# Two places for the query tiles, another order of score tiles, and new step times in an attention layer's hand-written order

## The chip, the cores and the metric

One NeuronCore of a Trainium2 chip runs the whole program. Its engines are TensorE (PE, with its weight loads as PEld), VectorE (DVE), ScalarE (ACT), GpSimd (POOL) and SyncE (SP), whose queue issues every DMA here. The metric is the device time of one execution in microseconds (us).

## The reference

A transformer layer on x of 2 x 1024 x 512: latent attention with 32 heads, then a gated feed-forward, each between layer norms and added to x. All in float32.

```
q = rms_norm(x @ wq_a.T, q_norm_w) @ wq_b.T            # 32 heads of 128 + 64
q_pe = rope(q[..., 128:]);  kv = x @ wkv_a.T
k_pe = rope(kv[..., 64:]);  k_nope, v = rms_norm(kv[..., :64]) @ wkv_b.T
scores = (q_nope . k_nope + q_pe . k_pe) * scale, causal
out = softmax(scores) @ v @ wo.T
x = x + layernorm(attn(layernorm(x)))
x = x + layernorm((silu(h @ w_gate.T) * (h @ w_up.T)) @ w_down.T)   # h = layernorm(x)
```

## The kernel before

Every float32 product is made of three on rounded halves (high x high, high x low, low x high; `three`). The attention works in the latent space: keys are 128 rows (64 latent, 64 rotary) shared by all heads, so each head needs its queries (two halves c of 512 tokens), its scores, its probabilities times the latents, and, per pair of heads, a transpose of the results that are then multiplied by a folded matrix of values and output weights.

A **job** is one tile of 128 queries of one head; there are 64 heads (2 batches x 32) of 8 jobs, in the order `TILES`. Tile j sees (j+1) x 128 keys. For a job PE makes the scores in one of four places of PSUM (`s_ps`: 1, 2, 2 and 1 banks, job i in place i % 4), DVE takes the `minimum` (L1371), ACT the `exponential` (L1168) and `split_high` (L1176, into pk), DVE `split_low` (L1384), after which the place is free for job i + 4. Two neighbouring jobs have 9 blocks of 128 x 128 together, a **pair** u; SP sends the pair through a transposing DMA from pk (NPK = 3 places) to pt (NPT = 4 places) (`turn_probs`, L772), PE multiplies it with the latents (`values`, L987, 18 matmuls of 130 columns into o_ps), DVE inverts the sums (`invert_sums`), ACT scales (`outputs_norm`, L1185), POOL adds two halves into o_pair (`outputs_add`, L1578), PE transposes them (`outputs_turn`, L996), and ACT and DVE split them into ot_high (L1194) and ot_low (L1391).

The queries of head n are made while head n - 1 runs. For each half PE makes a product (L116, x_ps<-qa...,weff_in), ACT copies it to q_raw (`queries_raw`, L1158), two DMAs of SP swap its rotary rows into qs (`queries_swap`, L782), and POOL turns and splits it in five steps (`queries_turn`): qf = raw x cos (L1548), qs = qs x sin (L1551), qf + qs (L1554), q_high (L1559), q_low (L1561). q_raw, qf and qs have one place each, so the second half waits for the first: ACT for the first half's cos and swap, SP for its L1554.

The products with the folded matrix (`output`, L116, x_ps<-m_in,ot...) come once for four heads (a group), eight of them, spread over the next group; their sums are taken by DVE (L1407) or ACT (L1213). In the second batch m_in is loaded again from memory, 1 MB for a group (`output_load`, L791); in the first it is made beside the heads (`fold_values`, L1004) and stored.

All products but scores and values go through one bank, x_ps, which each of them takes only when its predecessor was read (`take_bank`). Every engine executes its part of one list in order. The list is sorted by **steps**, one step a job: scores of job i stand at step i, everything else at a step plus a delay from the tables at the file's head. A line such as

```
for u in range(NJ // 2):
    at(2 * u + 1 + TURN_PROBS, "turn_probs", u)
    step = 2 * u + 1 + VALUES
```

puts the transpose of pair u behind its second job. A step says nothing of time: it only says what stands ahead of what in each engine's row. At the end the first token work of the feed-forward is mixed in between the last output products (EARLY_START, EARLY_EVERY).

Of the kernel before, what the change touches and what calls it, by code (L numbers as in the profile page):

```python
# [35 lines left out]
NX, NA, NPK, NPT, NON = 4, 3, 3, 4, 8  # L36
# [14 lines left out]
O_STEPS = (4.97, 7.03)
AFTER_OUTPUT = dict(output_add=0.36, output_store=1.5)
FOLD_STEP = 1.07
AFTER_FOLD = dict(fold_high=0.02, fold_low=1.08, fold_store=1.5)
END_STEP, END_EVERY = 9.71, 1.38
# [10 lines left out]
EARLY_START, EARLY_EVERY = 6.94, 0.84  # L66

PACES = (7, 3, 4)
# [12 lines left out]
TILES = (1, 6, 4, 3, 0, 7, 5, 2)  # L81
# [50 lines left out]
class Signals:  # L132


    def __init__(self, new):
# [23 lines left out]
        self.q_mm, self.q_raw, self.q_swap, self.q_cos, self.q_sin = (  # L159
            new(n) for n in ("q_mm", "q_raw", "q_swapped", "q_cos", "q_sin"))  # L160
# [268 lines left out]
def attention_order(end):  # L429
# [858 lines left out]
def vector_program(e, M, S):  # L1288
    w = Waits(e)
    def latents_begin():  # L1290
        e.memset(M.eps1[:, 0:1], LN_EPS)
# [218 lines left out]
def gpsimd_program(e, M, S):  # L1510
# [189 lines left out]
```

## Time and profile before

| | us |
|---|---|
| median of three executions | 1716.17 |
| lowest, highest | 1712.88, 1717.09 |
| the profiled execution, time | 1718.1 |
| its span | 1716.3 |
| PE busy | 1572.2 (92%) |
| DVE, ACT, POOL busy | 1147.7, 1069.0, 952.9 |

The span runs from the first instruction to the last; the time is 1.8 us longer. A share of busy time is a mean over stages: about 96 us that make the latents, then the attention, a change-over, and the feed-forward. Matmul records overlap their neighbours, so a PE that is called busy can still start its matmuls late.

### The profile page before, as it was taken

The numbers are of one execution on the slowest core, as the hardware profiler recorded it, in microseconds if no ns is written. First come the engines' busy times: TensorE is split into PE (matmuls) and PEld (weight loads), VectorE is DVE, ScalarE is ACT, GpSimd is POOL, SyncE is SP. The second block draws the span as 40 slices with busy tenths as digits, with TensorE's granted clock in tenths as the row PEclk, the third lists the DMA queues.
The fourth block names the chain that finished last, engine by engine and source line by source line (L and its number), as shares of the span: only waits on it lengthen the run. The fifth ranks groups of instructions, "written<-read, shape, count | busy, mean of one in ns | idle before, by whom it ended". The sixth has DMA issues, their size and how long they took to land.

```text
span 1716.3 us, 30452 instructions
## 1 busy us (share of the span) xinstructions
PE 1572.2 (92%) x10720; PEld 1275.9 (74%) x10720; DVE 1147.7 (67%) x2548; ACT 1069.0 (62%) x2159; POOL 952.9 (56%) x911
## 2 busy tenths in 40 slices
PE   5878999999998999998999999999978899999997
PEld 5856777778777777777877777777766677888775
DVE  6866677777777777776777777777766542323356
ACT  5677777777777777777877777777754433212122
POOL 2556677677676677676767677677622321111132
PEclk9899999999999999999999999999998999999998
DMA  8669999998999989899889898988996300201022
GB/s 280 227 140 206 164 200 181 189 200 174 203 175 190 180 190 201 184 187 188 171 172 190 164 179 169 183 171 165 184 186 239 121 25 1 74 1 39 1 92 80
DMA packets 661095, 268.84 MB, mean 157 GB/s; under 512 B 608432, under 2 KB 619184, under 8 KB 658768
## 3 DMA queue, kind: packets, MB, share of 16 engines
q1 hardware_dynamic: 660944, 266.90, 72.0%
q8 instruction: 86, 1.41, 0.3%
q14 instruction: 65, 0.53, 0.1%
HBM read 69.70 MB, written 29.36 MB: 58 GB/s over the span
## 4 chain that ended last, share of the span: by engine, by line
PE 56%; DMA 14%; DVE 11%; ACT 6%; POOL 6%; issue 4%; SPq 2%; POOLq 0%; ACTq 0%; DVEq 0%
PE f_ps L116 14%; PE s_ps L973 12%; PE x_ps L116 11%; DMA pt<-pk 10%; PE o_ps L987 9%; PE fd_ps L116 6%; DMA qs<-q_raw 3%; DVE pk L1384 3%; PE x_ps L996 2%; DVE s_ps L1371 1%; POOL q_low L1561 1%; POOL qf L1554 1%; POOL qs L1551 1%; SPq L772 1%; ACT ot_high L1194 1%
## 5 line engine op out<-in xcount | busy, mean ns | idle before, releaser
L1384 DVE SCALAR_TENSOR_TENSOR pk<-s_ps,pk 128x256 f16<-128x256 f32 (+7 forms) x512 | 383.7, 749 | 132.7 <-ACT pk L1176 132.4
L1168 ACT ACTIVATE s_ps<-s_ps,nbias 128x256 f32<-128x256 f32 (+7 forms) x512 | 371.3, 725 | 129.7 <-DVE nbias L1371 126.2
L1371 DVE CUSTOM_DVE_ANT_0 s_ps<-s_ps,far_sb 128x256 f32<-128x256 f32 (+7 forms) x512 | 388.4, 759 | 36.1 <-PE s_ps L973 30.9
L987 PEld LDWEIGHTS o_ps<-lat,pt 128*128 128x128 f16 x4608 | 268.2, 98 | 137.7 <-issue 70.4
L1176 ACT ACTIVATE pk<-s_ps 128x256 f16<-128x256 f32 (+7 forms) x512 | 339.6, 663 | 34.1 <-DMA pt<-pk 28.4
L987 PE MATMUL o_ps<-lat,pt 128*128 128x130 f16 x4608 | 312.0, 221 | 51.6 <-DMA pt<-pk 41.9
L1551 POOL TENSOR_TENSOR qs<-qs,sin_q 64x512 f32<-64x512 f32 x128 | 164.4, 1284 | 224.7 <-DMA qs<-q_raw 217.9
L973 PE MATMUL s_ps<-k_high,q_high 128*128 128x512 f32 (+3 forms) x768 | 283.6, 369 | 5.0 <-DVE k_low L1351 2.0
L973 PE MATMUL s_ps<-k_low,q_high 128*128 128x512 f32 (+3 forms) x768 | 257.1, 347 | 0.0
L1599 POOL TENSOR_TENSOR mid_low<-mid,mid_high 128x512 fp32r<-128x512 f32 (+1 forms) x44 | 57.2, 1300 | 303.1 <-ACT mid_high L1265 303.1
L973 PE MATMUL s_ps<-k_high,q_low 128*128 128x512 f32 (+3 forms) x768 | 224.3, 346 | 0.0
L1548 POOL TENSOR_TENSOR qf<-q_raw,cos_q 128x512 f32<-128x512 f32 x128 | 163.4, 1276 | 76.4 <-ACT q_raw L1158 65.7
L973 PEld LDWEIGHTS s_ps<-k_high,q_high 128*128 128x128 f32 x768 | 146.0, 190 | 34.9 <-POOL q_low L1561 9.3
L1561 POOL TENSOR_TENSOR q_low<-qf,q_high 128x512 fp32r<-128x512 f32 x128 | 164.6, 1286 | 10.3
L1554 POOL TENSOR_TENSOR qf<-qf,qs 64x512 f32<-64x512 f32 x128 | 164.0, 1281 | 10.0
L116 PE MATMUL x_ps<-m_in,ot_high 128*128 128x512 f32 x492 | 162.5, 411 | 2.3 <-DVE ot_low L1391 1.4
L1185 ACT ACTIVATE o_norm<-o_ps,rinv 128x128 f32<-128x128 f32 x512 | 159.7, 369 | 6.7 <-DVE rinv L1380 6.3
L973 PEld LDWEIGHTS s_ps<-k_low,q_high 128*128 128x128 f32 x768 | 146.6, 191 | 18.7
L116 PE MATMUL f_ps<-ft_high,w_high 128*128 128x512 f32 (+1 forms) x352 | 141.7, 403 | 6.6 <-DVE ft_low L1454 3.7
L1478 DVE TENSOR_TENSOR mid<-f_ps,gate 128x512 f32<-128x512 f32 (+1 forms) x44 | 30.3, 690 | 169.6 <-PE f_ps L116 156.9
L973 PEld LDWEIGHTS s_ps<-k_high,q_low 128*128 128x128 f32 x768 | 135.4, 190 | 8.1
L116 PE MATMUL f_ps<-ft_low,w_high 128*128 128x512 f32 (+1 forms) x352 | 140.9, 400 | 0.0
(134 smaller groups left out, 2622.1 us busy)
## 6 DMA issues: line engine op xcount, KB each, us to landing
weff_in<-weff SPq DMA_DIRECT2D x64, 256.0 KB, 3.2
qs<-q_raw SPq DMA_DIRECT2D x256, 64.0 KB, 2.1
weff<-weff_sb SPq DMA_DIRECT2D x8, 1024.0 KB, 5.3
wo_sb<-wo SPq DMA_DIRECT2D x16, 512.0 KB, 4.5
m_fold<-m_in SPq DMA_DIRECT2D x8, 1024.0 KB, 6.9
m_in<-m_fold SPq DMA_DIRECT2D x8, 1024.0 KB, 6.2
xin<-x SPq DMA_DIRECT2D x16, 256.0 KB, 4.7
wqn_sb<-wqn SPq DMA_DIRECT2D x8, 512.0 KB, 6.9
```

The costliest lines, as they stand in the source:

```text
L116: ins = e.matmul(out, stationary, moving, start=n == 0, stop=n == len(pairs) - 1)
L973: ins = e.matmul(s[:, c:c + width], queries[:, r, q], side[:, keys], start=queries is M.q_high and side is M.k_high, stop=queries is M.q_low)
L987: ins = e.matmul(M.o_ps[:, i % 2, :], M.pt[:, u % NPT, m, :], M.lat2[:, b * JT + (m - blocks[0]) // 2, :], start=m == blocks[0], stop=m == ...
L1168: e.activation(M.scores_of(i), M.scores_of(i), ACT.Exp, bias=M.nbias[:, i % 4:i % 4 + 1], scale=-1.0).then_inc(S.exp)
L1176: e.activation(M.halves_of(i)[:, :, 0, :], M.tiles_of(i), ACT.Copy, scale=P_SCALE).then_inc(S.p_high)
L1185: ins = e.activation(M.o_norm[:, r, :], M.o_ps[:, side, 0:P], ACT.Copy, scale=M.rinv[:, r:r + 1])
L1371: e.tensor_tensor_reduce(out=s, in0=s, in1=M.far_sb[:, SEQ - width:SEQ], scale=1.0, scalar=3e38, op0=ALU.add, op1=ALU.min, accum_out=M.nbi ...
L1384: e.scalar_tensor_tensor(out=M.halves_of(i)[:, :, 1, :], in0=M.tiles_of(i), scalar=P_SCALE, in1=M.halves_of(i)[:, :, 0, :], op0=ALU.mult, ...
L1548: e.tensor_tensor(M.qf[:, :], M.raw[:, :], M.cos_q[:, col], ALU.mult).then_inc(S.q_cos)
L1551: e.tensor_tensor(M.qs[KVL:P, :], M.qs[KVL:P, :], M.sin_q[KVL:P, col], ALU.mult).then_inc(S.q_sin)
L1554: e.tensor_tensor(M.qf[KVL:P, :], M.qf[KVL:P, :], M.qs[KVL:P, :], ALU.add).then_inc(S.q_turned)
L1561: e.tensor_tensor(M.q_low[:, n % 2, col], M.qf[:, :], f32(M.q_high[:, n % 2, col]), ALU.subtract).then_inc(S.q_split)
```

## The change

It changes these things:

- q_raw, qf and qs have two places each, one for each half of a head. ACT, SP and POOL wait for the place of the same half of the head before; the swap's semaphore becomes two.
- pt has five places instead of four. `values` stands 8.04 instead of 6.09 steps behind its pair, the transposes of the results later too.
- TILES goes through the tiles as 3 4 6 1 2 5 7 0, before 1 6 4 3 0 7 5 2. The output products now go in this order, two in each head of the next group.
- The rounding of the first weights (wa) is a turn of its own in the list, behind DVE's first statistics.
- All other step numbers are new.

```
-NX, NA, NPK, NPT, NON = 4, 3, 3, 4, 8
+NX, NA, NPK, NPT, NON = 4, 3, 3, 5, 8
-TURN_PROBS = 2.41
-VALUES = 6.09
+TURN_PROBS = 2.44
+VALUES = 8.04
-TURN_STEPS = (4.75, 4.72)
+TURN_STEPS = (6.26, 6.09)
-Q_STEPS = (0.0, 2.66)
-AFTER_QUERIES = dict(queries_raw=0.69, queries_swap=0.03, queries_turn=1.93)
+Q_STEPS = (0.84, 2.95)
+AFTER_QUERIES = dict(queries_raw=0.13, queries_swap=0.31, queries_turn=0.13)
...
-PACES = (7, 3, 4)
+PACES = (5, 3, 4)
...
-TILES = (1, 6, 4, 3, 0, 7, 5, 2)
+TILES = (3, 4, 6, 1, 2, 5, 7, 0)
...
-            self.raw = sb(attn, "q_raw", [P, 512])
-            self.qf = sb(attn, "qf", [P, 512])
-            self.qs = sb(attn, "qs", [P, 512])
+            self.raw = sb(attn, "q_raw", [P, 2, 512])
+            self.qf = sb(attn, "qf", [P, 2, 512])
+            self.qs = sb(attn, "qs", [P, 2, 512])
...
+    at(WEIGHT_STEPS[0], "weights_round")
+    at(WEIGHT_STEPS[1], "weights_rest")
...
-        for j in range(JT):
+        for m, j in enumerate(TILES):
             if g < N_GROUPS - 1:
-                step = GROUP_JOBS * (g + 1) + JT * (j // 2 + 1) + O_STEPS[j % 2]
+                step = GROUP_JOBS * (g + 1) + JT * (m // 2 + 1) + O_STEPS[m % 2]
             else:
-                step = NJ + END_STEP + END_EVERY * PLACE[j]
+                step = NJ + END_STEP + END_EVERY * m
...
     def queries_swap(n, c):
         k = 2 * n + c
         w.wait_ge(S.q_raw, k + 1)
-        if k:
-            w.wait_ge(S.q_turned, k)
+        if k >= 2:
+            w.wait_ge(S.q_turned, k - 1)
...
     def queries_raw(n, c):
-        if 2 * n + c:
-            w.wait_ge(S.q_cos, 2 * n + c)
-            w.wait_ge(S.q_swap, 2 * DMA * (2 * n + c))
-        e.activation(M.raw[:, :], bank, ACT.Copy).then_inc(S.q_raw)
+        if n:
+            w.wait_ge(S.q_cos, 2 * n + c - 1)
+            w.wait_ge(S.q_swap[c], 2 * DMA * n)
+        e.activation(M.raw[:, c, :], bank, ACT.Copy).then_inc(S.q_raw)
```

PE, in the second head of a group (head 41), around the first output transposes of that head. Before:

```order
L987 MATMUL o_ps<-lat,pt 128x130 x18
L996 MATMUL x_ps<-ident,o_pair 128x128 x4
L973 MATMUL s_ps<-k_high,q_high 128x512
L973 MATMUL s_ps<-k_low,q_high 128x512
L973 MATMUL s_ps<-k_high,q_high 128x128
L973 MATMUL s_ps<-k_low,q_high 128x128
L973 MATMUL s_ps<-k_high,q_low 128x512
L973 MATMUL s_ps<-k_high,q_low 128x128
L116 MATMUL x_ps<-qa_high,weff_in 128x512
```

After:

```order
L994 MATMUL o_ps<-lat,pt 128x130 x18
L1003 MATMUL x_ps<-ident,o_pair 128x128 x4
L980 MATMUL s_ps<-k_high,q_high 128x512
L980 MATMUL s_ps<-k_low,q_high 128x512
L980 MATMUL s_ps<-k_high,q_high 128x384
L980 MATMUL s_ps<-k_low,q_high 128x384
L980 MATMUL s_ps<-k_high,q_low 128x512
L980 MATMUL s_ps<-k_high,q_low 128x384
L118 MATMUL x_ps<-qa_high,weff_in 128x512
```

Between the transposes and the next user of x_ps stand the scores of a tile of 896 keys, where they were those of one with 640.

SP, at the load of a group's m_in in the second batch (pt<-pk are the transposes of probabilities, qs<-q_raw the swaps). Before:

```order
L772 DMA_TRANSPOSE pt<-pk 128x18x128
L757 DMA weff_in<-weff 128x512
L772 DMA_TRANSPOSE pt<-pk 128x18x128 x2
L782 DMA qs<-q_raw 32x512 x2
L791 DMA m_in<-m_fold 128x2048
L772 DMA_TRANSPOSE pt<-pk 128x18x128
L782 DMA qs<-q_raw 32x512 x2
```

After:

```order
L778 DMA_TRANSPOSE pt<-pk 128x18x128
L763 DMA weff_in<-weff 128x512
L778 DMA_TRANSPOSE pt<-pk 128x18x128
L798 DMA m_in<-m_fold 128x2048
L778 DMA_TRANSPOSE pt<-pk 128x18x128
L788 DMA qs<-q_raw 32x512 x2
```

The load moved from behind the first half's swap to ahead of a transpose and that swap; otherwise the row of SP is the same.

POOL, over one head. Before:

```order
L1548 TENSOR_TENSOR qf<-q_raw,cos_q 128x512
L1551 TENSOR_TENSOR qs<-qs,sin_q 64x512
L1554 TENSOR_TENSOR qf<-qf,qs 64x512
L1559 CAST q_high<-qf 128x512
L1561 TENSOR_TENSOR q_low<-qf,q_high 128x512
L1578 TENSOR_TENSOR o_pair<-o_norm 128x4x64
L1548 TENSOR_TENSOR qf<-q_raw,cos_q 128x512
```

After:

```order
L1570 TENSOR_TENSOR q_low<-qf,q_high 128x512
L1557 TENSOR_TENSOR qf<-q_raw,cos_q 128x512
L1560 TENSOR_TENSOR qs<-qs,sin_q 64x512
L1563 TENSOR_TENSOR qf<-qf,qs 64x512
L1568 CAST q_high<-qf 128x512
L1570 TENSOR_TENSOR q_low<-qf,q_high 128x512
L1587 TENSOR_TENSOR o_pair<-o_norm 128x4x64 x2
```

The two turns of a head now stand together, and both sums into o_pair behind them.

## Rows read from the trace of the kernel before

**Rows 1.** Windows by stage: busy us (instructions) of PE, PEld, DVE, ACT, POOL; clock, DMA.

```profile
96.00:1254.00 1158.00, 1082.12 (x8385) 878.80 (x8385) 863.21 (x1935) 873.45 (x1722) 813.24 (x753) 0.99 0.92 181
1254.00:1309.00 55.00, 39.06 (x266) 30.81 (x263) 39.49 (x85) 24.50 (x48) 9.16 (x10) 0.93 0.72 185
1309.00:1716.00 407.00, 382.02 (x1632) 303.36 (x1632) 173.94 (x295) 113.34 (x168) 90.12 (x68) 0.97 0.18 62
```

**Rows 2.** Timeline of PE: start, duration, instruction, idle before it and releaser.

```profile
96.21 0.55 PE L973 MATMUL s_ps<-k_high,q_high 128*128 128x256 f32 x1 [1.99 <-DVE k_low L1351]
...
1253.94 0.36 PE L973 MATMUL s_ps<-k_high,q_high 128*128 128x256 f32 x1
```

**Rows 3.** The same windows over single heads.

```profile
834.41:851.44 17.03, 16.94 (x139) 14.08 (x136) 12.51 (x30) 14.22 (x30) 12.61 (x13) 1.00 0.80 160
851.44:870.80 19.36, 17.21 (x139) 14.09 (x136) 13.43 (x32) 14.75 (x29) 13.32 (x13) 1.00 1.01 205
...
888.70:906.30 17.60, 17.06 (x137) 13.95 (x135) 13.78 (x32) 13.75 (x28) 12.64 (x12) 1.00 0.81 161
```

**Rows 4.** Waits of PE's matmuls, 97 to 1255 us: total, times, longest.

```profile
PE o_ps L987 <- DMA pt<-pk: 40.1, 34, 3.3
PE x_ps L116 <- DVE ot_low L1391: 13.1, 30, 0.4
PE x_ps L996 <- DVE m_in L1398: 5.4, 8, 0.9
PE x_ps L996 <- POOL o_pair L1578: 4.2, 8, 0.6
PE o_ps L987 <- ACT o_norm L1185: 4.2, 14, 0.4
PE x_ps L116 <- DMA weff_in<-weff: 3.1, 2, 1.6
PE s_ps L973 <- POOL q_low L1561: 1.6, 6, 0.3
```

**Rows 5.** Timeline of SP's queue over two heads.

```profile
842.96 1.77 SPq L782 DMA_DIRECT2D qs<-q_raw  x2
844.82 2.78 SPq L772 DMA_TRANSPOSE pt<-pk  x1
...
856.55 5.59 SPq L772 DMA_TRANSPOSE pt<-pk  x1
862.25 1.76 SPq L782 DMA_DIRECT2D qs<-q_raw  x2
```

**Rows 6.** Tile pt, 97 to 1255 us: a waiter (us, times), and landing.

```profile
  ACT pk L1176: 28.4, 18
...
DMA to landing us min/median/max: 4.6/4.8/9.6
```

**Rows 7.** Waits of SP's queue, 97 to 1255 us.

```profile
SPq L129 <- POOL qf L1554: 63.6, 49, 4.1
```

**Rows 8.** Timeline of POOL in the same two heads.

```profile
841.61 1.27 POOL L1554 TENSOR_TENSOR qf<-qf,qs 64x512 f32<-64x512 f32 x1
...
850.77 1.29 POOL L1561 TENSOR_TENSOR q_low<-qf,q_high 128x512 fp32r<-128x512 f32 x1
...
866.37 1.29 POOL L1551 TENSOR_TENSOR qs<-qs,sin_q 64x512 f32<-64x512 f32 x1 [2.06 <-DMA qs<-q_raw]
```

**Rows 9.** Timeline of PE behind the transposes of results.

```profile
856.40 0.40 PE L973 MATMUL s_ps<-k_low,q_high 128*128 128x512 f32 x1
856.63 0.22 PE L973 MATMUL s_ps<-k_high,q_high 128*128 128x128 f32 x1
...
857.74 0.50 PE L116 MATMUL x_ps<-qa_high,weff_in 128*128 128x512 f32 x1 [0.43 <-DVE ot_low L1391]
...
859.01 0.39 PE L973 MATMUL s_ps<-k_high,q_high 128*128 128x512 f32 x1
```

**Rows 10.** Timeline of DVE at the start.

```profile
10.88 0.69 DVE L1300 BATCH_NORM_STATS2 stats<-xin 128x6 f32<-128x512 f32 x1
```

More of the change, by code:

```diff
@@ L40 @@
 CW = 512
-AFTER_SCORES = dict(minimum=1.02, exponential=1.16, split_high=1.78, split_low=2.94)
-TURN_PROBS = 2.41
-VALUES = 6.09
-AFTER_VALUES = dict(invert_sums=1.31, outputs_norm=1.68, outputs_add=3.17)
-TURN_STEPS = (4.75, 4.72)
-AFTER_TURN = dict(outputs_high=0.0, outputs_low=0.96)
-Q_STEPS = (0.0, 2.66)
-AFTER_QUERIES = dict(queries_raw=0.69, queries_swap=0.03, queries_turn=1.93)
[L51 to L55, printed above, removed]
+AFTER_SCORES = dict(minimum=0.8, exponential=1.24, split_high=2.06, split_low=2.28)
+TURN_PROBS = 2.44
+VALUES = 8.04
+AFTER_VALUES = dict(invert_sums=1.21, outputs_norm=1.63, outputs_add=0.63)
+TURN_STEPS = (6.26, 6.09)
+AFTER_TURN = dict(outputs_high=0.27, outputs_low=0.95)
+Q_STEPS = (0.84, 2.95)
+AFTER_QUERIES = dict(queries_raw=0.13, queries_swap=0.31, queries_turn=0.13)
+O_STEPS = (3.4, 6.23)
+AFTER_OUTPUT = dict(output_add=1.26, output_store=1.5)
+FOLD_STEP = 1.03
+AFTER_FOLD = dict(fold_high=0.17, fold_low=1.03, fold_store=1.5)
+END_STEP, END_EVERY = 10.86, 3.22
 AFTER_TILE = dict(x_load=-2.13, statistics=-0.35, deviation=-0.05, normalise=0.81, transpose_x=1.12,
@@ L65 @@
 TABLES_STEP = 6.94
[L66 to L68 removed]
+WEIGHT_STEPS = (-0.5, 0.5)
+EARLY_START, EARLY_EVERY = 8.34, 2.51
+PACES = (5, 3, 4)
 LN_EPS, RMS_EPS = 1e-5, 1e-6
@@ L158, in __init__ @@
         self.weff_in = ring("weff_in", 2)
-        self.q_mm, self.q_raw, self.q_swap, self.q_cos, self.q_sin = (
-            new(n) for n in ("q_mm", "q_raw", "q_swapped", "q_cos", "q_sin"))
+        self.q_mm, self.q_raw, self.q_cos, self.q_sin = (
+            new(n) for n in ("q_mm", "q_raw", "q_cos", "q_sin"))
+        self.q_swap = ring("q_swapped", 2)
         self.q_turned, self.q_high, self.q_split = (
@@ L475, in attention_order @@
                 at(step + AFTER_OUTPUT["output_store"], "output_store", g, j)
-            if j == JT - 1 and NG <= g + 2 < N_GROUPS:
+            if m == JT - 1 and NG <= g + 2 < N_GROUPS:
                 at(step + 1, "output_load", g + 2)
@@ L778, in queries_swap @@
         w.wait_ge(S.q_raw, k + 1)
-        if k:
-            w.wait_ge(S.q_turned, k)
+        if k >= 2:
+            w.wait_ge(S.q_turned, k - 1)
         for to, at in ((KVL, KVL + HALF), (KVL + HALF, KVL)):
-            e.dma_start(M.qs[to:to + HALF, :], M.raw[at:at + HALF, :]).then_inc(S.q_swap, DMA)
+            e.dma_start(M.qs[to:to + HALF, c, :], M.raw[at:at + HALF, c, :]
+                        ).then_inc(S.q_swap[c], DMA)
     def output_store(g, j):
@@ L1547, in queries_turn @@
         w.wait_ge(*last)
-        e.tensor_tensor(M.qf[:, :], M.raw[:, :], M.cos_q[:, col], ALU.mult).then_inc(S.q_cos)
-        w.wait_ge(S.q_swap, 2 * DMA * (k + 1))
+        e.tensor_tensor(M.qf[:, c, :], M.raw[:, c, :], M.cos_q[:, col], ALU.mult).then_inc(S.q_cos)
+        w.wait_ge(S.q_swap[c], 2 * DMA * (n + 1))
         w.wait_ge(S.q_cos, k + 1)
-        e.tensor_tensor(M.qs[KVL:P, :], M.qs[KVL:P, :], M.sin_q[KVL:P, col], ALU.mult
+        e.tensor_tensor(M.qs[KVL:P, c, :], M.qs[KVL:P, c, :], M.sin_q[KVL:P, col], ALU.mult
                         ).then_inc(S.q_sin)
         w.wait_ge(S.q_sin, k + 1)
-        e.tensor_tensor(M.qf[KVL:P, :], M.qf[KVL:P, :], M.qs[KVL:P, :], ALU.add
+        e.tensor_tensor(M.qf[KVL:P, c, :], M.qf[KVL:P, c, :], M.qs[KVL:P, c, :], ALU.add
                         ).then_inc(S.q_turned)
```

11 lines of the change are left out of this document (6 added, 5 removed).

## The prediction

> **What bounds the kernel now.** I read the stages first [rows 1]. The attention takes 1158 of the 1716.3 us, and PE is busy for 1082.1 of them; the feed-forward takes 407 us with PE busy for 382.0. So PE sets the pace nearly everywhere, and the question is what makes it wait. DVE (863), ACT (873) and POOL (813 us busy of 1158) have room; the DMA share is 0.92, so the transfers have little.
>
> The first scores matmul starts at 96.21 and that of the last head at 1253.94 [rows 2]: 63 heads in 1157.7 us, 18.38 us a head. Three of four neighbouring heads show the spread [rows 3]: 17.03, 19.36 and 17.60 us, with almost the same PE work in each (16.94 to 17.21 us busy). A head can thus be done in 17.0 us. What the others lose is in PE's waits [rows 4]: 40.1 us in 34 waits for transposed probabilities (pt<-pk), 13.1 in 30 for ot_low, 5.4 in 8 for m_in, 4.2 for o_pair, 4.2 for o_norm, 3.1 for weff_in and 1.6 for q_low. Together 71.7 us, 1.14 us a head: 18.38 less that is 17.2, which agrees with the short heads. That sum is all that an order can win in the attention.
>
> Why do transposes come late? SP's queue shows it [rows 5]. A transpose undisturbed is issued in 2.78 us, and median 4.8 and at worst 9.6 us pass to its landing [rows 6]. The swap of the second half of the queries (qs<-q_raw at 842.96) starts only after POOL's add into qf ended (841.61 + 1.27 = 842.88), since qs has one place; the next transpose stands behind it, at 844.82. This kind of wait takes SP 63.6 us in 49 cases [rows 7]. In the head of 19.36 us a transpose behind the 1 MB load of m_in needs 5.59 us to issue, and the next swap waits until 862.25 [rows 5].
>
> **The change, part by part.** Durations are of the profiled execution: span 1716.3, time 1718.1 us, 1.9 above the median 1716.17.
>
> *Values two steps later, five places for pt.* A transpose of pair u stands at step 2u+3.41 and its product at 2u+7.09; now 2u+3.44 and 2u+9.04. The cover grows from 3.68 to 5.60 steps of 18.38/8 = 2.30 us: from 8.5 to 12.9 us, against 4.8 and 9.6 us. Every landing seen fits. The fifth place keeps the wait for its reader harmless: the place is freed by values(u-4), at step 2u+1.04, before the transpose at 2u+3.44. Of the 40.1 us I take 34 away and leave 6 for the start, where nothing is ahead, and for landings behind 1 MB transfers; bounds 0 and 40.1. What could be late next is pk, which keeps three places: ACT already waits 28.4 us for its reading [rows 6], off PE's path so far.
>
> The Trainium skill, in "Advanced Engine Details and Errata", X-Bar Transpose (TRN2), says that a transposing DMA is as fast as an ordinary one, at 350 to 400 GB/s. As an estimate from that page, the 0.59 MB of one (18 blocks of 128 x 128 in two bytes) would pass in about 1.6 us, no wait for pt would exist, this term would be 0 and the time 1708. The 40.1 us of waits [rows 4] contradict that and leave it no chance of its own; the sum goes by them.
>
> *Two places for raw, qf and qs.* This removes SP's wait for POOL (63.6 us, 1.0 a head [rows 7]) and lets ACT write q_raw of the second half at once. It is no term of its own: it brings forward the transpose behind the swap, which is in the 34. On POOL the second half no longer waits for its swap, 2.06 us at 866.37 [rows 8]; the first half still does. POOL is not the bound, so this counts only in o_pair's 4.2 and q_low's 1.6 us [rows 4].
>
> *Second output transposes moved.* Now they come in odd heads at steps 1.3 and 5.1; PE then goes on with the scores of tiles 6 and 7 (before: tile 5 in an even head, tile 4 in an odd one). After them x_ps must be emptied. Behind the transposes and tile 4's scores the query product waits 0.43 us for ot_low until 857.74 [rows 9]. Tile 6 has 896 columns instead of 640; each is passed three times, and 512 take 0.23 us (856.40 to 856.63), so its scores cover 3 x 256 / 512 x 0.23 = 0.35 us more. The wait of 0.44 (13.1 / 30) shrinks to 0.09: 30 x 0.35 = 10 us. Bounds 0 and 13.1, since ACT and DVE reach x_ps later if they are behind. The Trainium skill, in "Perfetto Trace Analysis", Matmuls, wants independent matmul groups in different PSUM banks. x_ps stays one bank, so by that page the wait would stay, this term would be 0 and the time 1684, within A below.
>
> *Order of tiles 3 4 6 1 2 5 7 0, output products in their order.* No instruction is added. In each pair there are still nine blocks, and DVE still runs minimum two jobs ahead of split_low. The products of output move by some steps and each still has scores or a product of values before the next user of x_ps. o_pair: both sums now stand behind both query turns on POOL. The second turn of a head ends by about 17 us after its start (850.77 + 1.29 in the head from 834.41 [rows 8] is 17.65 with a sum of 0.73 and a second wait inside it, both gone now), and PE needs the sum over 3 us into the next head, behind two tiles of scores, a query product (1.27 us from 857.74 to 859.01 [rows 9]) and a product of values: the 4.2 us go. m_in's 5.4 stays, since fold_values still stands right before the transposes in every fourth head. weff_in and o_norm are kept, but 1 us for the later first query product. Term: 5 us.
>
> *What may come new.* Swap and transposes stand in the same sequence on SP, but the 1 MB load of m_in moves ahead of a transpose and the next first-half swap. Its excess was 19.36 - 17.6 = 1.8 us in its head; eight loads at up to 1 us against the present cost, 0 to 8 us; and the pipeline is two products longer, 2 x 1.03 us when it drains. I take 8 us for all new waits, bounds 0 and 30.
>
> *Start, end, feed-forward.* The rounding of wa no longer delays DVE's first statistics: 10.88 to 11.70 [rows 10] goes into the wait for wa before it: 1 us. Behind the attention the output sums now stand ahead of the token work, and less of that work is mixed in; PE is idle for 16 of 55 us there [rows 1], and DVE has the same work in it. I take 0, bounds -8 and +8. The pace of 5 instead of 7 moves three pieces of the last blocks; PE has no wait for them: 0.
>
> Sum: 34 + 10 + 5 + 1 - 8 = 42 us. 1718.1 - 42 = 1676.1, against the median 1716.17 - 42 = **1674**.
>
> **Rivals.**
> *B, the transfers hold it.* The DMA share is 0.92 over the attention, 1.01 in the head with the m_in load, 0.80 and 0.81 in the others [rows 1, 3]. If 0.94 is all that can be sustained, a head needs 18.38 x 0.92 / 0.94 = 17.99 us, 0.39 less: 63 x 0.39 = 25 us, **1691**. Against it: 0.80 in a head of 17.0 us says that packets aren't the limit there.
> *C, nothing is gained.* ACT's wait for a place of pk (28.4 us) takes over what PE no longer waits, because three places stay: **1716**. Against it: transposes are issued earlier, not later.
> *D, slower: the queries come late.* The chain is first query product, q_raw, swap, five POOL steps, twice. In the head from 834.41 it ends at 852.06. If raw and swap were delayed so that the second q_low ends after scores of the next head's second job would start (now tile 4, behind tile 3 with three times 512 columns at 0.23 and the query product of 1.27: 1.96 us in), PE waits in every head. With heads of 17.1 us it decides from 19 us after the head's start; 17 is what I expect. At 0.7 us over, 63 x 0.7 = 44 us more, with the gain on transposes hidden under it: **1760**. For it: q_low makes PE wait already (1.6 us), and the m_in load now delays a first swap. Against it: a second wait of 2 us is gone.
> *E, all waits go* and the drain is covered: 1716.2 - 71.7 = **1644**.
>
> **How the numbers follow.** A (1674) 0.57, with its own range 1655 to 1695; B 0.13; C 0.08; D 0.12; E 0.10. 1674 is the likeliest. The range 1642 to 1712 holds A, B and E and leaves out C and D, 0.20 together. A measurement can tell 0.3%, 5 us, from no change: faster A, B, E 0.80; same 0.08; slower 0.12.
>
> **What would show it.** PE's wait for pt below 8 us in the attention, heads near 17.7 us on average (18.38 - 42 / 63), and SP without a wait for qf. The wait for ot_low near 3 us. POOL's long waits for qs<-q_raw in first halves alone. Waits of ACT for pt<-pk above 40 us would speak for C, PE's for q_low above 20 us for D, and a DMA share of 0.94 or less with heads near 18 us for B. I am wrong at the root if PE has few waits left and heads still take 18.3 us.

## The result

The changed kernel takes **1672.85 us** (median of 4 runs, 1665.7 to 1673.47) against 1716.36 us for the kernel before, measured beside it. The ratio is 0.9741 (95% interval 0.9711 to 0.977): 43.5 us less, and the forecast was 42. The profiled execution of after is its fastest, 1665.7 us with a span of 1663.9, so differences between the two traces are up to 9 us larger than the one between the medians.

The page of after gives the span and the engines' busy time, the engines' shares in the chain that ended last, and the group that had PE's largest idle time before.

```profile
span 1663.9 us, 30455 instructions
...
PE 1554.2 (93%) x10720; PEld 1287.8 (77%) x10720; DVE 1150.5 (69%) x2548; ACT 1079.8 (65%) x2159; POOL 954.1 (57%) x911
...
PE 66%; DVE 10%; POOL 8%; ACT 6%; DMA 6%; issue 3%; SPq 2%; POOLq 0%; ACTq 0%; DVEq 0%
...
L994 PE MATMUL o_ps<-lat,pt 128*128 128x130 f16 x4608 | 309.3, 220 | 8.5 <-ACT o_norm L1192 8.5
```

The same two rows of the page of before:

```profile
PE 56%; DMA 14%; DVE 11%; ACT 6%; POOL 6%; issue 4%; SPq 2%; POOLq 0%; ACTq 0%; DVEq 0%
...
L987 PE MATMUL o_ps<-lat,pt 128*128 128x130 f16 x4608 | 312.0, 221 | 51.6 <-DMA pt<-pk 41.9
```

DMA's share of that chain was 14% before and is 6% now. Ahead of the products of values (L987 before, L994 now) PE stood idle for 51.6 us in the old kernel, 41.9 of them for the transposes, and for 8.5 us in the new one, all of them for o_norm: no transfer is among the releasers any more.

The windows by stage, cut at the first scores, at those of the last head and at the first gate matmul (columns as in [rows 1]), and below them three single heads:

```profile
93.30:1196.40 1103.10, 1066.35 (x8361) 893.51 (x8362) 861.14 (x1931) 882.48 (x1719) 812.50 (x752) 0.99 0.97 190
1196.40:1249.50 53.10, 39.33 (x289) 30.80 (x286) 40.70 (x88) 26.30 (x52) 11.04 (x11) 0.93 0.77 202
1249.50:1663.90 414.40, 383.38 (x1632) 304.23 (x1632) 177.38 (x294) 113.34 (x168) 90.16 (x68) 0.97 0.17 60
```

```profile
803.29:819.32 16.03, 16.03 (x135) 14.02 (x132) 12.09 (x30) 14.31 (x29) 12.49 (x12) 1.00 0.90 165
819.32:836.85 17.53, 17.33 (x143) 14.68 (x140) 13.77 (x30) 14.56 (x29) 11.17 (x11) 1.00 1.09 212
836.85:853.39 16.54, 16.29 (x134) 13.97 (x132) 13.30 (x31) 13.59 (x27) 13.89 (x15) 1.00 1.05 189
```

From first scores to the last head's, 63 heads take 1103.1 us, 17.51 a head, where they took 1157.7 us [rows 2]: **54.6 us less**. PE's idle time there fell from 75.9 us [rows 1] to 36.8 (1103.10 - 1066.35). The feed-forward, which was forecast to stay, takes **7 us more**: 414.4 against 407.4 us. The same head as in [rows 3], with the 1 MB load of m_in in front of or in it, takes 17.53 us (the middle row), where it took 19.36.

PE's waits from 97 to 1255 us, as in [rows 4]. That window ended with the attention before; now its last 59 us lie behind it:

```profile
PE s_ps L980 <- POOL q_low L1570: 9.7, 15, 1.5
PE x_ps L118 <- DMA weff_in<-weff: 9.5, 8, 2.1
PE o_ps L994 <- ACT o_norm L1192: 8.5, 12, 1.8
PE x_ps L118 <- DVE ot_low L1400: 7.3, 31, 1.7
...
PE x_ps L1003 <- DVE m_in L1407: 4.2, 8, 0.5
...
PE s_ps L980 <- DVE pk L1393: 2.0, 2, 1.1
```

In the attention alone (97 to 1196.4 us) they are weff_in 9.5 us (8 waits), q_low 9.3 (14), ot_low 5.5 (30), o_norm 4.9 (9), m_in 4.2 (8) and pk 2.0 (2), and these are the figures to hold against [rows 4]. The row on top there, 40.1 us for pt<-pk, is gone, and so is o_pair's 4.2; ot_low fell from 13.1. Two waits grew: q_low (1.6 before) and weff_in (3.1); o_norm (4.2) hardly did. The same window for SP's queue, and for the tile pt (a waiter, and the time from issue to landing), to be held against [rows 7] and [rows 6]:

```profile
SPq L778 <- DVE pk L1393: 563.3, 243, 6.3
SPq L788 <- ACT q_raw L1165: 17.6, 29, 3.1
```

```profile
  ACT pk L1183: 9.3, 18
...
DMA to landing us min/median/max: 4.5/4.8/9.3
```

In the attention SP no longer waits for POOL at all (63.6 us before). A transpose lands as late as before, median 4.8 and at worst 9.3 us: the transfer didn't get faster, it got cover, that is, more steps between its issue and its product.

### The profile page after: what moved, and what is told of

Read it like the earlier page. It is cut to its first block, busy times and chain, and to the rows that moved or that the text cites. A ratio compares the mean times of both kernels' runs of the same rounds, so it can differ in the third digit from the quotient of the medians.

```text
span 1663.9 us, 30455 instructions
## 1 busy us (share of the span) xinstructions
PE 1554.2 (93%) x10720; PEld 1287.8 (77%) x10720; DVE 1150.5 (69%) x2548; ACT 1079.8 (65%) x2159; POOL 954.1 (57%) x911
## 4 chain that ended last, share of the span: by engine, by line
PE 66%; DVE 10%; POOL 8%; ACT 6%; DMA 6%; issue 3%; SPq 2%; POOLq 0%; ACTq 0%; DVEq 0%
PE s_ps L980 16%; PE x_ps L118 15%; PE f_ps L118 13%; PE o_ps L994 11%; PE fd_ps L118 6%; POOL qf L1563 2%; POOL q_low L1570 2%; DMA qs<-q_raw 2%; DMA pt<-pk 2%; POOL qs L1560 2%; DMA weff_in<-weff 2%; PE x_ps L1003 2%; ACT ot_high L1201 1%; DVE f_stats L1435 1%; SPq L778 1%
## 5 line engine op out<-in xcount | busy, mean ns | idle before, releaser
L1393 DVE SCALAR_TENSOR_TENSOR pk<-s_ps,pk 128x512 f16<-128x512 f32 (+7 forms) x512 | 386.0, 754 | 116.2 <-ACT pk L1183 114.3
L1175 ACT ACTIVATE s_ps<-s_ps,nbias 128x512 f32<-128x512 f32 (+7 forms) x512 | 366.2, 715 | 90.6 <-DVE nbias L1380 81.8
L1380 DVE CUSTOM_DVE_ANT_0 s_ps<-s_ps,far_sb 128x512 f32<-128x512 f32 (+7 forms) x512 | 387.8, 757 | 44.4 <-PE s_ps L980 44.2
L1183 ACT ACTIVATE pk<-s_ps 128x512 f16<-128x512 f32 (+7 forms) x512 | 336.1, 656 | 14.9 <-DMA pt<-pk 9.3
L994 PE MATMUL o_ps<-lat,pt 128*128 128x130 f16 x4608 | 309.3, 220 | 8.5 <-ACT o_norm L1192 8.5
L994 PEld LDWEIGHTS o_ps<-lat,pt 128*128 128x128 f16 x4608 | 265.2, 97 | 41.5 <-issue 33.9
L980 PE MATMUL s_ps<-k_high,q_high 128*128 128x512 f32 (+3 forms) x768 | 279.2, 364 | 13.8 <-POOL q_low L1570 9.7
L980 PEld LDWEIGHTS s_ps<-k_high,q_high 128*128 128x128 f32 x768 | 145.4, 189 | 44.6 <-POOL q_low L1570 18.6
```

The source lines that it names most:

```text
L980: ins = e.matmul(s[:, c:c + width], queries[:, r, q], side[:, keys], start=queries is M.q_high and side is M.k_high, stop=queries is M.q_low)
L994: ins = e.matmul(M.o_ps[:, i % 2, :], M.pt[:, u % NPT, m, :], M.lat2[:, b * JT + (m - blocks[0]) // 2, :], start=m == blocks[0], stop=m == ...
L1175: e.activation(M.scores_of(i), M.scores_of(i), ACT.Exp, bias=M.nbias[:, i % 4:i % 4 + 1], scale=-1.0).then_inc(S.exp)
L1183: e.activation(M.halves_of(i)[:, :, 0, :], M.tiles_of(i), ACT.Copy, scale=P_SCALE).then_inc(S.p_high)
L1380: e.tensor_tensor_reduce(out=s, in0=s, in1=M.far_sb[:, SEQ - width:SEQ], scale=1.0, scalar=3e38, op0=ALU.add, op1=ALU.min, accum_out=M.nbi ...
L1393: e.scalar_tensor_tensor(out=M.halves_of(i)[:, :, 1, :], in0=M.tiles_of(i), scalar=P_SCALE, in1=M.halves_of(i)[:, :, 0, :], op0=ALU.mult, ...
```

## The experiments

The stages of every trace, in us, with the median and the ratio to the kernel before (95% interval). The ratios are to the kernel before on the same chip (medians 1713.5 to 1716.4 us); by them the distance to after is 3 to 6 us larger than between the medians: 20 us for cover_back_exact, 47 for one_place, 33 for tiles_old.

| kernel | to first scores | attention (a head) | change-over | feed-forward | median | ratio |
|---|---|---|---|---|---|---|
| before | 96.2 | 1157.7 (18.38) | 55.0 | 407.4 | 1716.36 | 1 |
| after | 93.3 | 1103.1 (17.51) | 53.1 | 414.4 | 1672.85 | 0.9741 |
| before_two | 93.9 | 1153.6 (18.31) | 56.1 | 405.6 | 1710.52 | 0.9973 (0.9956 to 0.999) |
| before_cover | 96.0 | 1409.5 (22.37) | 56.1 | 405.5 | 1962.67 | 1.146 (1.1422 to 1.1499) |
| before_cover_two | 97.1 | 1391.0 (22.08) | 56.6 | 405.8 | 1957.12 | 1.1437 (1.1389 to 1.1486) |
| before_cover_fitted | 93.9 | 1178.7 (18.71) | 57.4 | 406.8 | 1740.56 | 1.0149 (1.0111 to 1.0186) |
| cover_back | 94.0 | 1149.8 (18.25) | 57.9 | 415.8 | 1714.42 | 1.0011 (0.9989 to 1.0033) |
| cover_back_exact | 93.3 | 1120.6 (17.79) | 56.7 | 416.0 | 1687.7 | 0.986 (0.9812 to 0.9907) |
| one_place | 93.3 | 1151.2 (18.27) | 55.2 | 414.8 | 1715.25 | 1.0013 (0.9996 to 1.003) |
| tiles_old | 95.9 | 1135.8 (18.03) | 53.7 | 414.3 | 1702.98 | 0.9933 (0.9906 to 0.9959) |
| paces_back | 97.4 | 1104.7 (17.53) | 54.6 | 405.8 | 1662.83 | 0.9697 (0.967 to 0.9723) |
| paces_back_m_in_later | 95.5 | 1099.0 (17.44) | 55.3 | 405.9 | 1657.51 | 0.9668 (0.9642 to 0.9695) |
| paces_back_weff_earlier | 93.6 | 1101.6 (17.49) | 53.5 | 405.4 | 1658.18 | 0.9684 (0.9648 to 0.9721) |
| paces_back_both | 94.6 | 1096.6 (17.41) | 56.3 | 406.8 | 1656.42 | 0.9663 (0.9641 to 0.9685) |

### The cover of the transposes, taken back

**cover_back**, from after:

```diff
-NX, NA, NPK, NPT, NON = 4, 3, 3, 5, 8
+NX, NA, NPK, NPT, NON = 4, 3, 3, 4, 8
-VALUES = 8.04
-AFTER_VALUES = dict(invert_sums=1.21, outputs_norm=1.63, outputs_add=0.63)
-TURN_STEPS = (6.26, 6.09)
+VALUES = 6.09
+AFTER_VALUES = dict(invert_sums=1.21, outputs_norm=1.63, outputs_add=2.58)
+TURN_STEPS = (8.21, 8.04)
```

> The changed kernel with values back at 6.09 steps and four places for pt; the sums into o_pair and the output transposes keep their steps. Theory of the prediction (the cover of 5.6 steps took the 40.1 us of waits for pt): PE's waits for pt come back, 25 to 35 us over the attention, and the time is 1698 to 1708 us. Rival (the second places for the queries let SP issue the transposes early enough by themselves): waits for pt below 8 us, time 1673 to 1680.

Measured: 1714.42 us, above both forecasts, the whole gain gone; but pt is less than half of it. In the attention PE waits 20.6 us (23 times) for pt and 24.8 us (56) for o_norm. The step 6.09 put `invert_sums` at .30 of a step, just behind `split_low` at .28 on DVE (in after it stands at .25, ahead of it), and ACT's scaling waited 111.9 us for rinv. So this run mixes two causes: the cover, and the inversion's place behind `split_low`. **cover_back_exact** removes the second: VALUES 6.04 leaves every fraction of a step as in after.

```diff
-VALUES = 8.04
-AFTER_VALUES = dict(invert_sums=1.21, outputs_norm=1.63, outputs_add=0.63)
-TURN_STEPS = (6.26, 6.09)
+VALUES = 6.04
+AFTER_VALUES = dict(invert_sums=1.21, outputs_norm=1.63, outputs_add=2.63)
+TURN_STEPS = (8.26, 8.09)
```

(and NPT = 4 again)

> The changed kernel with values exactly one pair (2.00 steps) earlier, at 6.04, and four places for pt; sums and transposes of results keep their steps. In the earlier run with 6.09 the inversion of sums came to stand behind split_low on DVE, and ACT waited 111.9 us for it; here every engine's row is that of the changed kernel but for the one pair. If the cover alone is what counts: PE waits for pt about 20 us and for nothing else new, time 1690 to 1698. If the place among the steps did it too (rival: most of the 42 us were lost to the inversion behind split_low): below 1685.

Measured: 1687.7 us, 15 us above after and between the two forecasts (1690 to 1698, and below 1685). So the larger part of what cover_back lost, 27 us, was not the cover. PE's waits from 97 to 1255 us:

```profile
PE o_ps L994 <- DMA pt<-pk: 32.1, 32, 2.8
PE o_ps L994 <- ACT o_norm L1192: 8.4, 16, 1.8
...
PE x_ps L1011 <- ACT q_raw L1165: 3.3, 4, 0.9
...
PE s_ps L980 <- POOL q_low L1570: 0.9, 2, 0.7
```

The wait for pt is back almost whole, 32.1 us (one of its 32 waits lies behind the attention, which holds 30.6), but the attention is only 17.5 us longer than in after. The difference is paid by two rows: weff_in (9.5 us in after) has none here, and q_low has 0.9 for 9.3. 30.6 + 3.3 - 9.5 - 8.4 = 16.0 us, and PE's idle time in the attention is 16.6 us larger (53.3 against 36.7). So what after waits for q_low and weff_in is waiting that the late transposes had covered. It is not a defect of the new order as such. The fifth place of pt was taken away together with the two steps; what it is worth by itself no run shows.

### The cover alone, put into the kernel before

**before_cover**, from before:

```diff
-NX, NA, NPK, NPT, NON = 4, 3, 3, 4, 8
+NX, NA, NPK, NPT, NON = 4, 3, 3, 5, 8
-VALUES = 6.09
+VALUES = 8.04
```

> The kernel before with two numbers changed: VALUES 8.04 and five places for pt. Theory of the prediction: the wait for pt falls from 40.1 to 6 us and the time to 1680 to 1686 (its term of 34 us). Rival (order of tiles and the queries matter as much, so that another wait takes over): 1700 to 1716.

Measured: 1962.67 us, 246 us slower, which neither forecast foresaw. No row for pt is left, and two others stand on top, from 97 to 1255 us:

```profile
PE x_ps L996 <- POOL o_pair L1578: 108.2, 47, 3.8
PE x_ps L116 <- DVE ot_low L1391: 52.2, 49, 1.2
```

This attention lasts until 1505.5 us, and over all of it the two are 139.4 us (58 waits) and 63.1 us (59). `VALUES` takes the sum o_pair and PE's transposes of it along by the same 1.95 steps, while the queries keep theirs. So one of the sums, at 0.26 of a head's eight steps before, now stands at 2.21, behind a whole turn of the queries (1.93) on POOL, and PE's transposes come at 3.76. The timeline of POOL, of PE, and 4 us windows around the place (columns as in [rows 1]):

```profile
610.11 1.26 POOL L1561 TENSOR_TENSOR q_low<-qf,q_high 128x512 fp32r<-128x512 f32 x1
611.52 0.72 POOL L1578 TENSOR_TENSOR o_pair<-o_norm 128x256 f32<-128x256 f32 x1
```

```profile
612.29 0.92 PE L996 MATMUL x_ps<-ident,o_pair 128*128 128x128 f32 x4 [2.24 <-POOL o_pair L1578]
...
614.62 1.22 PE L116 MATMUL x_ps<-m_in,ot_high 128*128 128x512 f32 x2 [0.88 <-DVE ot_low L1391]
...
617.35 0.63 PE L973 MATMUL s_ps<-k_high,q_high 128*128 128x512 f32 x1
617.78 0.63 PE L973 MATMUL s_ps<-k_low,q_high 128*128 128x512 f32 x1
```

```profile
608.00:612.00 4.00, 2.06 (x23) 1.53 (x21) 1.84 (x5) 2.20 (x4) 3.64 (x4) 1.00 0.96 178
612.00:616.00 4.00, 2.83 (x10) 2.42 (x11) 1.69 (x4) 2.75 (x7) 1.51 (x2) 0.57 1.06 339
616.00:620.00 4.00, 4.00 (x16) 2.96 (x15) 1.41 (x3) 0.53 (x3) 3.59 (x4) 0.58 0.66 166
620.00:624.00 4.00, 4.00 (x35) 3.42 (x33) 2.45 (x7) 2.79 (x5) 1.60 (x2) 1.00 0.80 147
...
96.00:1505.50 1409.50, 1179.18 (x8366) 955.53 (x8367) 866.27 (x1934) 872.53 (x1719) 811.32 (x753) 0.91 0.75 149
```

POOL ends the turn at 611.37 and only then adds; PE has stood for 2.24 us. The granted clock then falls to 0.57 and 0.58 for 8 us, near the lower of its two levels (1.2 of 2.4 GHz): 0.43 us pass from one matmul of 512 columns to the next (617.78 less 617.35), where they were 0.23 [rows 9]. Over the attention the clock is 0.91 (0.99 before) and PE is busy for 1179 us with the work that took 1082; 1082 x 0.99 / 0.91 = 1177, so the clock accounts for that. So of the 252 us by which this attention is longer, 97 are a PE busier with the same work and 155 are waiting: **each us of waiting cost 1.6 us** in this run, because the clock fell with it. **before_cover_two** is the same with two places for raw, qf and qs:

> The kernel before with VALUES 8.04, five places for pt, and two places for q_raw, qf and qs. Theory of the prediction: as with the cover alone or up to 4 us less, 1677 to 1686. Rival (second places are worth as much as the cover): 15 us or more below the run with the cover alone. What is left to 1672.85 belongs to the order of tiles and the other steps.

Measured: 1957.12 us, o_pair 100.5 us (48) in the same window. The two places change little (the intervals of the ratios overlap): the order on POOL, which they leave as it is, still holds PE.

**before_cover_fitted** gives before all the step times of after that go with the results: the fifth place of pt, but not two places for queries, not the tile order.

```diff
-VALUES = 6.09
-AFTER_VALUES = dict(invert_sums=1.31, outputs_norm=1.68, outputs_add=3.17)
-TURN_STEPS = (4.75, 4.72)
-AFTER_TURN = dict(outputs_high=0.0, outputs_low=0.96)
-O_STEPS = (4.97, 7.03)
+VALUES = 8.04
+AFTER_VALUES = dict(invert_sums=1.21, outputs_norm=1.63, outputs_add=0.63)
+TURN_STEPS = (6.26, 6.09)
+AFTER_TURN = dict(outputs_high=0.27, outputs_low=0.95)
+O_STEPS = (3.4, 6.23)
```

(also NPT = 5, output_add at 1.26, the outputs in the order of the tiles, and END and EARLY as in after)

> The kernel before (its order of tiles, query steps, one place for the queries) with values at 8.04, five places for pt, and all that hangs on it placed as in the changed kernel: sums into o_pair, transposes of results, outputs in the order of tiles. The wait for pt should be gone. If the cover is the main thing: 1680 to 1692. If second places and query steps are needed for it: 1700 or more, with the time in waits for q_raw or q_low.

Measured: 1740.56 us, still 24 us slower than before, as the second forecast had it. The wait for pt is gone and others have come: q_raw 28.3 us (32), ot_low 24.0 (59), m_in 13.3 (8), weff_in 7.6 (11). Even with the results' steps as in after, the cover alone gains nothing; all four of these waits stand before users of x_ps.

### Two places for the queries

**before_two**, from before, adds only these places, with the waits of after:

```diff
-            self.raw = sb(attn, "q_raw", [P, 512])
-            self.qf = sb(attn, "qf", [P, 512])
-            self.qs = sb(attn, "qs", [P, 512])
+            self.raw = sb(attn, "q_raw", [P, 2, 512])
+            self.qf = sb(attn, "qf", [P, 2, 512])
+            self.qs = sb(attn, "qs", [P, 2, 512])
```

> The kernel before with two places for q_raw, qf and qs and no other edit. Prediction's theory (no term of its own): SP's wait for qf goes, 63.6 us, transposes of the third pair of a head are issued about 1 us earlier, the wait for pt falls by a few us, time 1708 to 1716. Rival after the run with one place (they carry the gain): 1690 or less.

Measured: 1710.52 us, 0.9973. SP's wait for qf (63.6 us [rows 7]) is gone, and its wait for q_raw has grown from 15.1 to 47.7 us; PE's wait for pt in the attention falls from 40.1 [rows 4] to 34.9 us. In the old order this part is worth 4 us, as the prediction's theory had it.

**one_place** takes the same places out of after, with the old waits:

```diff
-        if k >= 2:
-            w.wait_ge(S.q_turned, k - 1)
+        if k:
+            w.wait_ge(S.q_turned, k)
...
-        if n:
-            w.wait_ge(S.q_cos, 2 * n + c - 1)
-            w.wait_ge(S.q_swap[c], 2 * DMA * n)
+        if 2 * n + c:
+            w.wait_ge(S.q_cos, 2 * n + c)
+            w.wait_ge(S.q_swap[1 - c], 2 * DMA * (n + c))
```

(and raw, qf and qs indexed with 0)

> The changed kernel with one place for q_raw, qf and qs and the old waits; order and all else as changed. Theory of the prediction (no term of its own once values stand far behind): SP waits for POOL's qf again, about 60 us, but PE's waits for pt stay below 8 us, and the time is 1673 to 1680. Rival (the second places carry the gain, since the new steps place the second half so early): the second q_low comes late, PE waits for q_low 20 us or more, and the time is 1690 or more.

Measured: 1715.25 us: in the new order the same part is worth **42 us**, ten times as much. The rival was right in the time and wrong in the wait: q_low has 0.6 us in the attention, and the row on top is one that neither forecast named. PE's largest waits, then one stall as SP's queue, ACT, PE and the windows show it:

```profile
PE x_ps L118 <- ACT q_raw L1165: 31.6, 18, 4.3
PE x_ps L118 <- DMA weff_in<-weff: 18.6, 14, 3.0
```

```profile
774.23 0.53 SPq L798 DMA_DIRECT2D m_in<-m_fold  x1
774.85 6.00 SPq L778 DMA_TRANSPOSE pt<-pk  x1
...
781.57 1.16 SPq L788 DMA_DIRECT2D qs<-q_raw  x2
```

```profile
784.23 0.60 ACT L1165 ACTIVATE q_raw<-x_ps 128x512 f32<-128x512 f32 x1 [4.10 <-DMA qs<-q_raw]
```

```profile
784.97 1.19 PE L118 MATMUL x_ps<-m_in,ot_high 128*128 128x512 f32 x2 [4.09 <-ACT q_raw L1165]
```

```profile
780.00:800.00 20.00, 15.87 (x108) 13.20 (x106) 10.07 (x25) 11.79 (x24) 11.84 (x12) 0.83 0.91 180
```

The 1 MB load holds the transpose behind it (6.00 us to issue instead of 2.8), this holds the swap of the first half, the swap holds the only place of raw, ACT can't empty x_ps into it, and PE can't start the next product in x_ps. Over the 20 us that hold the wait of 4.09 us the clock is 0.83. This is no single case: behind each of the eight loads of m_in, 10 to 12 us after it, PE waits 1.4 to 4.3 us for q_raw, 24.2 of the 31.6 us. All but 1.4 us of the 31.6 lie in the second batch, where alone these loads stand; from 700 us on the clock is 0.97 (in after 1.00). With two places ACT has the other one, and the chain ends at the swap. Of the 48.1 us by which this attention is longer than in after, 33.5 are idle time of PE and the other 14.7 a PE busier with the same work; weff_in's wait, 18.6 for 9.5 us, which falls mostly in the first batch, has 9 of the 33.5, and q_low gives 9 back.

### The order of the tiles

**tiles_old**, from after:

```diff
-TILES = (3, 4, 6, 1, 2, 5, 7, 0)
+TILES = (1, 6, 4, 3, 0, 7, 5, 2)
```

> The changed kernel with the old order of tiles, 1 6 4 3 0 7 5 2. If the order is worth little (prediction: part of a term of 5 us): 1672 to 1680. Rival: the order spreads PE's work so that the softmax engines keep up, and without it the time is 1695 or more, with PE waiting for pk or q_low.

Measured: 1702.98 us, 30 us above after, with the attention 32.7 us longer. The rival was again right in the time and not in the wait: no row of PE names pk or q_low with more than 3.4 us. PE's waits from 97 to 1232 us:

```profile
PE x_ps L118 <- DVE ot_low L1400: 23.9, 59, 0.4
PE x_ps L118 <- DVE acc L1416: 13.8, 48, 0.4
```

Against after's 5.5 (30) for ot_low and no row for acc in the attention these are 18.4 + 13.8 = 32.2 us more. q_low and weff_in are 7.5 us less, so that PE's idle time is 24.5 us larger (61.2 against 36.7); the other 8.2 us of the 32.7 are a longer busy time. Each wait is short, 0.3 to 0.4 us on average, and the one for ot_low comes in nearly every head. That the new order sets larger scores in front of the users of x_ps is my reading for it; the run shows that the order of tiles and output products does it, not which tile.

### The pace of the last blocks, and the two loads

**paces_back**, from after:

```diff
-PACES = (5, 3, 4)
+PACES = (7, 3, 4)
```

> The changed kernel with PACES (7, 3, 4) as before. In the traces so far the feed-forward took 405.5 to 407.4 us with a pace of 7 and 414.3 to 416.0 with 5, whatever the attention was. If the pace is the cause: feed-forward 405 to 408 us and time 1663 to 1667. If the end of the attention leaves it another start (rival; prediction: no term): 414 us and 1672.

Measured: 1662.83 us, 10 us below after (7.5 by the ratios, whose intervals just overlap, so that the stages have to decide). The attention is the same (1104.7), the feed-forward is 8.6 us shorter. Its window, and the wait of PE's weight loads from 1540 us to the end, of paces_back, then of after:

```profile
1256.70:1662.50 405.80, 380.49 (x1632) 302.24 (x1632) 173.41 (x294) 113.28 (x168) 90.14 (x68) 0.97 0.18 61
```

```profile
PEld fd_ps L118 <- DVE f_acc L1495: 7.5, 10, 1.4
```

```profile
PEld fd_ps L118 <- DVE f_acc L1495: 13.9, 12, 3.4
```

PE's matmuls wait for f_acc in the same stretch too, 3.4 us in paces_back and 9.5 in after. Every trace with a pace of 5 shows 414.3 to 416.0 us for the feed-forward, every trace with 7 shows 405.4 to 407.4. The three last kernels keep the pace of 7 and move the load of m_in from 1 to 3 steps behind the last output product, the load of weff_in from 1 to 0.4 steps behind its products, or both:

```diff
-                at(step + 1, "output_load", g + 2)
+                at(step + 3.0, "output_load", g + 2)
```

> As paces_back, with the load of a group's m_in behind the swap of the next head's first half, as in the kernel before, instead of ahead of a transpose and that swap. If the load ahead of the swap costs as my term of new waits says (up to 8 us): PE's wait for q_low falls from 9.7 us to below 4 and the attention is 2 to 6 us shorter. If the two places and the cover absorb it either way: within 2 us of paces_back.

```diff
-            at(step + 1, "queries_load", n + 1)
+            at(step + 0.4, "queries_load", n + 1)
```

> As paces_back, with the load of the next head's query weights behind the second swap and ahead of the third transpose, one place earlier on SP. If the wait of 9.5 us for weff_in comes from the load standing behind a transpose: it goes, and the attention is 5 to 10 us shorter. If the transpose that is pushed back costs as much (rival: waits for pt return): no change or longer.

> Both moves of the loads with PACES as before: the candidate that should beat both kernels. Expected 1652 to 1662 us if both waits are real, 1664 if neither is.

Measured: 1657.51, 1658.18 and 1656.42 us, against 1662.83 for paces_back. The first gains 5 us by the medians and 5.7 in the attention; its four executions all lie below the four of paces_back, though the intervals of the ratios overlap. But the wait that was to fall below 4 us, q_low, falls only from 9.4 to 7.9 (weff_in from 10.9 to 6.9, while o_norm grows), and PE's idle time in the attention falls by 2.5 us alone. So the way by which the gain was expected isn't shown. In the second the wait for weff_in is gone, and the one for q_low is 18.8 us (17) for paces_back's 9.4: an earlier product only meets the queries sooner. Its attention is 3.1 us shorter, not 5 to 10, and its executions (1655.91 to 1667.7) overlap those of paces_back, so a gain isn't shown. Together they give the lowest median of the study, 0.9663 of before. Its attention, and its waits from 97 to 1255 us:

```profile
94.60:1191.20 1096.60, 1061.28 (x8363) 893.16 (x8363) 857.47 (x1931) 879.04 (x1718) 811.65 (x751) 1.00 0.99 191
```

```profile
PE s_ps L980 <- POOL q_low L1570: 15.3, 15, 2.7
PE o_ps L994 <- ACT o_norm L1192: 10.3, 14, 1.8
PE x_ps L118 <- DVE ot_low L1400: 7.3, 31, 1.7
```

The first and the last of these medians are 1.1 us apart, as far as single executions of one of them; that both moves are better than one isn't shown.

## Why the prediction came out right, step by step

The total was right, 42 us against 43.5: the waits for pt went, as the largest term said. But that the sum came so near is in good part luck. The attention gave 14 us more in the traces than its terms (54.6 against 41), 16 of its 54.6 us are a shorter busy time of PE that stands in no term, and the feed-forward took 7 back. And the terms are not what the parts are worth: taken out of after, the part priced at 34 us costs 15, one that got no term costs 42, and one that shared a term of 5 costs 30. (The stages of the two traces add up to 52.4 us; 7 of them because after's profiled execution is that far below its median, 2 because before's is above.)

- **Waits for pt: -34, measured -40.1, all of them.** I had left 6 us for the start and for landings behind 1 MB loads. The worst landing is 9.3 us, against a cover of 5.60 steps of 17.51 / 8 = 2.19 us, 12.3 us, and none was late. (One reading in this term was wrong and harmless: with five places, a place is freed by values(u-5), at step 2u-0.96; values(u-4) at 2u+1.04 holds for four.) But removing this wait is not worth its size: taken back exactly it costs 15 us by the medians and 17.5 in the attention (20 by the ratios), since PE, once faster, meets q_low and weff_in. The step that failed is to subtract a wait's sum from the span as if nothing stood behind it.
- The estimate of 1.6 us worked out from the rate in the Trainium skill, "Advanced Engine Details and Errata", X-Bar Transpose (TRN2), stays refuted: the transposes land after 4.5 us at best in after too, and cover_back_exact waits for them again. What failed is to take a rate for a landing time. The page's other statement, that a transposing DMA is as fast as an ordinary one, isn't contradicted here: in after the ordinary load of 256 KB from memory (weff_in) lands after a median of 3.2 us and that of 1 MB (m_in) after 6.2, on either side of the 4.8 us for 0.59 MB.
- **Two places: "no term of its own".** True for the kernel before, where the part alone gives 4 us (before_two). False for after, where it carries 42 us (one_place). I followed the wait of SP that it removes and not ACT's, which holds x_ps. Why ACT meets a late swap in the new order and not in the old is my reading: `queries_raw` now stands only 0.13 of a step behind its product (0.69 before), the two halves stand 2.11 steps apart (2.66), and the load of m_in stands ahead of the first-half swap. The runs don't separate these three. I even named the load of m_in that moves ahead of the first-half swap, and priced it at 1 us in each of 8 heads, without asking who is queued behind that swap if there is one place.
- **ot_low: -10, measured -7.6.** 30 waits of 0.44 us became 30 of 0.18 in the attention (13.1 to 5.5 us), so each gave 0.25 us where 0.35 was worked out. The direction was right. The Trainium skill's rule in "Perfetto Trace Analysis", Matmuls, to rotate PSUM banks, would have left the 13.1 us in place; x_ps is still one bank and the wait is 5.5.
- **Tile order, 5 us with o_pair's wait.** o_pair's 4.2 us went, as said. But the order of the tiles is worth 30 us (tiles_old), in ot_low and in products of output that wait for `output_add`. The trace of before shows little of this as a loss ([rows 4] has 13.1 us for ot_low and nothing for acc); that the old order fitted the old steps is my reading.
- **New waits: +8, bounds 0 and 30.** In the attention q_low grew by 7.7 us, weff_in by 6.4 and o_norm by 0.7: 14.8 us. The bounds hold it. Putting the load of m_in, the cause that was named, behind the swap again gives 5 us (paces_back_m_in_later), of which idle time of PE is 2.5; so most of the new waits come from elsewhere. q_low is the mechanism of rival D, which turned up in 14 heads, far from every head.
- **PE's busy time, not in the sum.** Of the 54.6 us, 39 are idle time of PE; its busy time also fell, by 16 us, with the same matmuls. So "all that an order can win", the 71.7 us of waits, was no bound. The granted clock from 96 to 196 us rose from 0.93 to 0.97, which I estimate at 4 us (0.04 of 100). What the other 12 are is open; PE's ends are modelled, and its busy time in before_two, one_place and tiles_old (1084.6, 1081.0, 1074.6 us) is roughly the longer, the more it waits.
- **Paces: 0, measured -8.6 by going back.** "PE has no wait for them" looked at too little: the step moves pieces of work among DVE and ACT, and the weight loads' wait for f_acc rises from 7.5 to 13.9 us, and that of the matmuls from 3.4 to 9.5. The change as a whole hid this loss.
- **Start -1, change-over 0.** Traces show -2.9 and -1.9, but the stretch to the first scores is 93.3 to 97.4 us in traces whose code is the same there (after and paces_back), so neither can be put down to the change.
- **Rivals.** B supposed that the DMA share can't pass 0.94; it is 0.97 over the attention and 1.09 in the head with m_in's load, with 17.53 us for that head. C supposed that ACT would wait for pk: 28.4 us fell to 9.3. E was nearer for pt than A was, but its other waits stayed. Of A's signs three held: no wait for pt, heads of 17.5 us (17.7), no wait of SP for qf. Two didn't: ot_low has 5.5 us where about 3 was said, and POOL's long waits for the swap are not in first halves alone. Second halves still wait 16 times in the trace of after, 40.5 us in all (18 times, 37.2 us before), so the "second wait of 2 us" that was to go did not.

The parts don't add up. Taken out of after one at a time, three of them cost 15, 42 and 30 us, 87 together, double the gain; put into before, two places give 4 us and the cover costs 24 (fitted) or 246. So the new order has to be judged as one design. For the cover, the trace shows how a part hides waits of another (q_low and weff_in); for the other two it is my reading.

**Open:** what the fifth place of pt, the new Q_STEPS and AFTER_QUERIES are worth alone wasn't tried, nor one place with the load of m_in moved away from the swap, nor what moves 8.6 us in the feed-forward instruction by instruction.

## What to carry to other kernels

In a kernel whose engines follow one list of steps, judge a part by what is queued behind it on every engine in the new order, not by the wait that it removes in the old one: a second buffer that looks idle in the trace of before can be the one that keeps a late transfer from reaching the bottleneck. Undo a part from the new kernel and do it alone in the old one; where the two results differ, as 42 and 4 us here, the parts belong together. And split both spans at fixed instructions, since a gain of 55 us in one stage hid a loss of 7 to 9 in another, which one number gave back.

## What the hardware showed unexpectedly

- Around a wait of PE of 4.1 us the clock was 0.83 over 20 us (one_place); behind two of 2.2 and 0.9 us it was 0.57 and 0.58 over 8 us (before_cover). There PE is busy for 97 us more with the same work, of 252 in all.
- The DMA engines' mean share reached 0.97 over 1103 us and 0.99 in paces_back_both, without a PE wait for pt. A share of 0.92 was no sign of a limit.
- Behind the plain 1 MB load on the same queue a transpose took 5.59 us (before), 5.73 (after) and 6.00 us (one_place) to issue, against 2.8 us undisturbed. All eight loads of each of these three traces show it, with 5.3 to 6.7 us for the next transpose.
